# One comparison of VectorE moved in front of four box additions in a four-layer convolution kernel

## The reference

```python
x = x + L0(gn(x))   # 1x1 convolution, weights mixed per image from 8 experts by a sparsemax gate
x = x + L1(gn(x))   # depthwise 3x3, BN, relu, prune; pointwise 1x1, BN, relu, prune
x = x + L2(gn(x))   # attention with squared, normalised queries and keys
x = x + L3(gn(x))   # 3x3 box mean, each channel by itself
```

```python
amax = jnp.max(jnp.abs(x), axis=(2, 3), keepdims=True)
return jnp.where(amax < thresh, jnp.zeros_like(x), x)
```

## Time and profile before

| what | value |
|---|---|
| median of three runs | 1683.83 us (1683.47 to 1685.27) |
| the profiled execution, its own time | 1683.19 us |
| its span, first to last instruction | 1681.4 us |
| mean granted TensorE clock | 0.972 of full speed |
| busy: TensorE, VectorE, ScalarE, GpSimd | 1543.4, 1452.5, 1369.0, 421.4 us |
| instructions of VectorE, GpSimd | 2530, 269 |

### The profile page before, as it was taken

How to read it: one execution, slowest core, us unless ns; L and a number is a source line. 1 busy time by engine, 2 the same in 40 slices (tenths; PEclk the granted TensorE clock), 3 DMA queues, 4 the chain that set the end, 5 groups by cost and what they waited for, 6 DMA issues and landing times. The chain is left out here.

```text
span 1681.4 us, 26750 instructions
## 1 busy us (share of the span) xinstructions
PE 1543.4 (92%) x8190; PEld 1144.9 (68%) x8190; DVE 1452.5 (86%) x2530; ACT 1369.0 (81%) x3496; POOL 421.4 (25%) x269
## 2 busy tenths in 40 slices
PE   3569999999999999999999999999999999998994
PEld 2247777677777767777776777777677777766773
DVE  5867799999989999998999999899999989998646
ACT  3368988888888888888888888888888888878872
POOL 1111212233321223332122333212233321223224
PEclk8689999999999999999999999999999999999997
DMA  4000011100111110011111001111100111000000
GB/s 143 20 20 20 20 39 39 39 20 20 39 38 38 38 38 19 19 38 38 38 38 38 19 19 38 38 38 38 38 19 19 38 38 39 20 20 20 20 20 39
DMA packets 21058, 55.58 MB, mean 33 GB/s; under 512 B 2321, under 2 KB 3345, under 8 KB 21010
## 3 DMA queue, kind: packets, MB, share of 16 engines
q1 hardware_dynamic: 20914, 54.98, 9.3%
q10 hardware_dynamic: 96, 0.00, 0.0%
HBM read 29.29 MB, written 25.69 MB: 33 GB/s over the span
## 5 line engine op out<-in xcount | busy, mean ns | idle before, releaser
L769 DVE SCALAR_TENSOR_TENSOR h<-xpad,dw_sb,h 128x784 f32<-128x784 f32 x512 | 534.3, 1097 | 1.1
L540 PE MATMUL tile_ps<-wqk,xn_parts 128*112 128x512 f32 x1344 | 363.6, 425 | 0.0
L540 PEld LDWEIGHTS tile_ps<-wqk,xn_parts 128*112 128x112 f32 x1344 | 234.6, 175 | 80.2
L1223 POOL TENSOR_SCALAR xpad<-x,gn_r,gn_s 128x784 f32<-128x784 f32 x64 | 64.8, 1020 | 784.1 <-DVE gn_s L700 784.1
L448 PE MATMUL conv_ps<-h,pw_masked 128*128 128x392 f32 x512 | 183.5, 502 | 42.6 <-DVE x L805 37.1
L582 PE MATMUL tile_ps<-k,xT 112*128 112x256 f32 x896 | 205.1, 388 | 7.7 <-ACT xT L1029 7.7
L582 PEld LDWEIGHTS tile_ps<-k,xT 112*128 112x128 f32 x896 | 174.2, 195 | 40.1 <-issue 8.4
L963 ACT ACTIVATE junk<-x 128x784 bf16<-128x784 f32 x192 | 163.1, 851 | 40.6 <-DVE x L805 20.7
L570 PE MATMUL conv_ps<-x,mixed 128*128 128x392 f32 (+1 forms) x512 | 177.4, 499 | 2.2 <-ACT mixed L997 1.1
L448 PEld LDWEIGHTS conv_ps<-h,pw_masked 128*128 128x128 f32 x512 | 93.4, 192 | 111.6 <-DVE x L805 38.7
L448 PE MATMUL conv_ps<-xn_parts,w_out 128*128 128x392 f32 x768 | 153.1, 348 | 0.0
(11 more groups left out here) (143 smaller groups left out, 3020.5 us busy)
## 6 DMA issues: line engine op xcount, KB each, us to landing
x<-x SPq DMA_DIRECT2D x32, 784.0 KB, 4.3
out<-x SPq DMA_DIRECT2D x32, 784.0 KB, 3.5
expert_sb<-expert_rows SPq DMA_DIRECT2D x8, 256.0 KB, 5.5
x<-w_qk SPq DMA_DIRECT2D x1, 512.0 KB
x<-w_vT SPq DMA_DIRECT2D x1, 256.0 KB
x<-w_ln SPq DMA_DIRECT2D x1, 256.0 KB
pw_sb<-pw_wT SPq DMA_DIRECT2D x1, 256.0 KB
gmean<-group_mean SPq DMA_DIRECT2D x1, 64.0 KB, 4.0
```

Source lines behind the costliest of these rows:

```text
L540: mm = nc.tensor.matmul(bank, xn2_parts[:, u, i, m * TOK:(m + 1) * TOK], wqk[:, v, i, :], start=False, stop=(i == J - 1 and u == 1))
L769: ins = nc.vector.scalar_tensor_tensor(acc, view, scalar, acc, ALU.mult, ALU.add)
```

## The change

In VectorE's `step` the call of `h_mask(C_)` is placed ahead of the call of `box_sums(F, ...)`. Nothing else is touched: the same instructions with the same operands, semaphores and counts, and the orders of the other engines stay.

```diff
                 if B.active:
                     depthwise(B, slice(1, 3))
+                if C_.active:
+                    h_mask(C_)
                 if F.active:
                     box_sums(F, range(BOX_STEPS))
-                if C_.active:
-                    h_mask(C_)
                 if B.active:
                     depthwise(B, slice(3, 5))
```

## The result

The changed kernel takes 1693.54 us (median of 4 runs, 1691.18 to 1694.46) where the kernel before takes 1683.65 in the runs beside it: a ratio of 1.0057, 95% interval 1.0039 to 1.0074, 9.9 us slower. The forecast was 1691.0, slower by 7.2. The profiled execution took 1691.18 us, its span is 1689.4, 8.0 longer than before.

The account below looks back on a forecast made before the run. VectorE was taken as the bound up to make_x3, without slack. 27 steady steps at +0.20 us (5.4), step 32 (1.4) and step 33 (0.4) gave +7.2 on 1683.83, so 1691.0 us; range 1685.5 to 1695.

Parts of the forecast that it names:

- P3: The first of GpSimd's last two box additions in a step; the moved comparison was to end 0.03 us behind it.
- The early mask: Masks 3 us earlier at TensorE's pointwise matmuls; gain taken as 0, bounded by 0.07 us per step.
- The moved comparison: VectorE's 0.16 us mask comparison, now ahead of its box additions; forecast +0.02 us a step, bounds 0 and +0.5.
- D1: VectorE's first box addition; forecast to take the lock before P4 and end 0.92 us behind P3 instead of 0.84.
- P4: GpSimd's last box addition, with the masking queued behind it; forecast to come after D1.
- M1 and M2: The two halves of GpSimd's weight masking; forecast to run among VectorE's additions, together +0.18 us a step.
- D2, D3 and D4: VectorE's second to fourth box additions; D3 and D4 forecast at about 1.06 to 1.1 us each instead of 0.98.
- Steps 32 and 33: Last two masked steps, where ScalarE's late sum holds back the comparison and additions; forecast +1.4 and +0.4 us.
- Rival 1: VectorE keeps the lock from D2 to D4, masking waits: +2.0 us, 1685.9 us; chance 0.15.
- Rival 2: Both masking halves run in one lock hold among the additions: +17.2 us, 1701.0 us; chance 0.08.
- Rival 3: ScalarE's sum comes late and the comparison holds up steady-step additions: +20.7 us, 1704.5 us; chance 0.05.
- Rival 4: Faster: small savings at TensorE and the comparison, masking starved, late steps half price: -2.9 us, 1680.9 us; chance 0.05.

Follow-up runs that it names:

- the two kernels with fills: GpSimd's masking replaced by constant fills, in the changed and the old order, against the kernel before: 1682.36 us (0.9995) and 1682.14 us (0.9991).
- the masking held back: The change, with GpSimd's masking also waiting for VectorE's fourth box addition, against the kernel before: 1687.51 us, ratio 1.0036.
- seven such taps in a row: make_x3 moved to right behind x2_low, comparison left behind the additions, against the kernel before: 1733.82 us, ratio 1.0299.

## Why the prediction was right, point by point

- *VectorE's make_x3 sets the step, and what it loses the step loses.* Right: +0.33 us at make_x3, +0.29 in the step. Every segment from make_x3 round to the next P3 keeps its length within 0.02 us; together they give back 0.04.
- *The early mask gives TensorE nothing.* Right: the wait is still make_x3's, and larger.
- *The moved comparison costs 0.02 us.* Confirmed by the two kernels with fills, whose orders differ by 0.01 us a step. That it would stand about 1.85 us behind P3 and end just behind it is what the profile shows (1.84, 0.02 us). D1 came before P4, as forecast.
- *M1 and M2 get in between D2, D3 and D4.* Right as a mechanism, and this is the term that was mis-sized: it was put at 0.27 + 0.83 = 1.10 us from end to end, +0.09 for each. Measured are 1.18 and 1.17, +0.17 and +0.16, since the masking's share of the lock is 0.35 us here and not 0.27. The 0.27 was read where M1 had waited out two taps. Wherever a masking instruction waited out only one VectorE instruction, an addition or a tap, it ended 0.35 us behind it, in each kernel here and in step 18 with the masking held back too. So the term was taken from a pattern that the additions do not have. Why the two differ is open. So a steady step costs 0.29 in place of 0.20, and 27 of them 7.7 us in place of 5.4.
- *Steps 32 and 33 add 1.8 us.* Too much. The comparison waited for ScalarE's sum in step 32 as forecast,

```profile
1535.69 1.30 DVE L777 TENSOR_SCALAR hmask<-h_over 128x2 f32<-128x2 f32 x1 [2.31 <-ACT over L1075]
```

  and make_x3 came 1.2 us later there (1.4 forecast). This was not all handed on: in step 32 of the kernel before, VectorE waited 1.15 us for TensorE's group statistics, as its timeline shows,

```profile
1558.43 0.17 DVE L686 COPY gn_avg<-small_ps 128x16 f32<-128x16 f32 x1 [1.15 <-PE small_ps L432]
```

  and this cover took a part; the statistics came 0.55 us later. Of step 33 nothing is left there. The kernels with fills agree: their orders differ by 0.2 us in all. I had taken the rule of the steady steps, no slack, into steps that have another one.
- *Rival 1, the masking starved:* it did not happen, M1 and M2 took 1.19 us each and got in at each gap. Two taps in a row mostly kept the masking out, but no run kept it out for longer. *Rival 2, one hold:* D3 took 1.14 us in the steady steps, never 1.5. *Rival 3, the late sum:* ScalarE's sum was in time in all steady steps. *Rival 4:* no sign of it.
- *Two slips.* The lower end of the forecast's own range, at 0.12 a step, is 27 x 0.12 + 1.8 = 5.0, which gives 1688.9 and not 1688.5. And where the opening says that the engines meet only through semaphores, VectorE and GpSimd also meet without one: the comparison takes 1.84 us behind P3, 0.16 where nothing stands beside it.

The rule of the Trainium skill ("SBUF — State Buffer", Who interferes with whom) that a VectorE instruction with two SBUF inputs meets a GpSimd instruction that reads SBUF, and not one that only writes it, agrees with the fills: two in 0.55 us while D2 ran. Its rule that the one to issue first gets the lock does not fit the taps: M1, waiting since 0.3 us behind the start of the first, came after the second in the kernel before (1.94 us).

The sizes add up to 7.7 us for the steady steps and about half a microsecond for step 32, 8.3. The timed runs gave 9.9 and 9.2, with intervals of about 6.6 to 12.5 and 7.6 to 13.0. Whether the last microsecond is real is open. That the forecast's total came near has some luck in it: the steady steps cost 2.3 us more than it had and the last ones 1.3 less.

## What to carry to other kernels

Between VectorE and GpSimd the question for an instruction is not only whether it is on the critical path, but what stands beside it: the masking behind two taps and beside make_x3, which reads PSUM, was free, and between additions each half cost VectorE 0.16 us. So releasing off-path work on GpSimd earlier can cost time, and in these kernels work that reads PSUM was what to put beside GpSimd. Two edits can be bad alone and good together, since each changes who stands beside whom.

## What the runs showed of the hardware that was not expected

- Two VectorE taps that overlap (the second starts 0.09 us before the first ends) mostly, not always, keep a waiting GpSimd instruction out: in 27 of 27 steady steps of the kernel before, in 15 of 27 with the masking held back, where it starts as far behind the first tap (0.30 or 0.41 us; 0.30 or 0.39 in the kernel before). What decides is open.
- They never kept it out for longer than two: with seven such taps in a row, M1 got in behind the second in 27 of 27 steady steps (1.84 to 1.94 us) and M2 behind the next (1.18).
- One and the same GpSimd instruction (128x256, one tile read) ended 0.27 us behind the VectorE instruction that it had waited for when it had waited out two taps, and 0.35 when it had waited out one tap or one addition. VectorE's own rows agree: among the seven taps the third ended 0.14 us late, behind M1, and the fourth 0.22, behind M2.
- A VectorE instruction of 128x2, 0.16 us long by itself, stood 1.84 us behind a GpSimd addition: being small does not let it past.
